# A graph network's first layer: its scatter-add goes to two tables in HBM in place of four

## What is computed

```
gate = sigmoid(edge_feature @ W_edge + b_edge)[:, 0]
xp = x @ W_node.T + b_node
row, col = src, dst
msg = gate[:, None] * xp[col]
summed = segment_sum(msg, row, num_segments=12500)
cnt = segment_sum(ones, row, num_segments=12500)
x = layernorm(x + summed / max(cnt, 1.0))
```

## Time and profile before

| | us |
|---|---|
| median of 3 runs | 13932.11 |
| lowest and highest | 13918.93 and 13973.37 |
| span of the profiled execution | 13968.9 |
| of it, first start of a scatter (L691) | 218.3 |
| last start of a scatter | 3319.1 |
| last of the three adds of the tables ends | 3364.5 |

### The profile page before, as it was taken

How to read it: one execution, slowest core, us unless ns; L and a number is a source line. 1 busy time by engine, 2 the same in 40 slices (tenths; PEclk the granted TensorE clock), 3 DMA queues, 4 the chain that set the end, 5 groups by cost and what they waited for, 6 DMA issues and landing times.

```text
span 13968.9 us, 160913 instructions
## 1 busy us (share of the span) xinstructions
PE 6562.6 (47%) x39606; PEld 5620.6 (40%) x39607; DVE 6528.4 (47%) x13212; ACT 1918.5 (14%) x3205; POOL 8846.4 (63%) x8158
## 2 busy tenths in 40 slices
PE   5777787784555555688600000085333333333333
PEld 5777777774555555677500000074111111111111
DVE  6444444444566666799700000198344345434335
ACT  0111111111222222566400000000000000000000
POOL 3888888884677777200177777500777774777774
PEclk7666666665777777899755555598555556555556
DMA  5333333332444444333222222232111111111111
GB/s 99 18 18 18 18 18 18 18 18 58 119 127 126 125 127 126 109 99 98 62 49 54 54 54 54 54 97 74 39 39 39 39 39 38 39 39 39 39 39 31
DMA packets 851731, 827.56 MB, mean 59 GB/s; under 512 B 630365, under 2 KB 636739, under 8 KB 849108
## 3 DMA queue, kind: packets, MB, share of 16 engines
q0 software_dynamic: 450064, 387.16, 18.7%
q1 hardware_dynamic: 398412, 436.75, 9.9%
q10 hardware_dynamic: 3218, 3.20, 0.1%
HBM read 571.36 MB, written 255.06 MB: 59 GB/s over the span
## 4 chain that ended last, share of the span: by engine, by line
POOL 51%; issue 22%; PE 10%; DMA 9%; DVE 5%; SPq 1%; DVEq 1%; POOLq 0%; ACT 0%; ACTq 0%
POOL tab L734 21%; POOL aux L708 10%; POOL lane_tab L691 9%; DMA lane_tab<-rows,idx 8%; POOL buf_b L708 6%; POOL acc_w L708 4%; PE ps L1122 3%; PE ps L1233 2%; PE ps L1169 1%; PE ps L1155 1%; DVE buf_b L1700 1%; SPq L558 1%; PE ps L1011 1%; POOL t_first_tab L719 1%; PE ps L1118 1%
## 5 line engine op out<-in xcount | busy, mean ns | idle before, releaser
L734 POOL DMA_INDIRECT tab<-gcn_tab,idx x3136 | 2984.5, 952 | 1780.3 <-issue 1777.6
L691 POOL DMA_INDIRECT lane_tab<-rows,idx x1664 | 2595.7, 1560 | 616.1 <-issue 614.6
L1134 PE MATMUL ps<-ident_b,zero_b 128*128 128x512 bf16 x1664 | 771.6, 618 | 2918.8 <-issue 1620.3
L1774 DVE TENSOR_REDUCE buf_d<-ps 128x512 f32<-128x1536 f32 x416 | 731.2, 1758 | 2301.0 <-PE ps L1138 2301.0
L708 POOL DMA_INDIRECT aux<-att_tab,idx x1568 | 1485.7, 948 | 477.8 <-issue 477.8
L1134 PEld LDWEIGHTS ps<-ident_b,zero_b 128*128 128x128 bf16 x1664 | 182.0, 128 | 3281.1 <-issue 1886.4
L708 POOL DMA_INDIRECT buf_b<-src_tab,idx x832 | 842.7, 1013 | 464.9 <-issue 253.4
L1036 PE MATMUL ps<-ident,srcg 128*128 128x128 f32 x3328 | 713.9, 401 | 663.4 <-DVE srcg L1398 663.3
L708 POOL DMA_INDIRECT acc_w<-src_tab,idx x832 | 815.4, 980 | 253.6 <-issue 248.1
L1036 PEld LDWEIGHTS ps<-ident,srcg 128*128 128x128 f32 x3328 | 661.0, 304 | 711.5 <-DVE srcg L1398 711.4
L1212 PE MATMUL ps<-ident,acc_w 128*128 128x128 f32 x13 | 3.0, 426 | 1953.9 <-ACT idx L831 1953.9
(11 more groups left out here) (307 smaller groups left out, 14192.6 us busy)
## 6 DMA issues: line engine op xcount, KB each, us to landing
y_stash<-buf_c SPq DMA_DIRECT2D x208, 512.0 KB
tab<-y_stash SPq DMA_DIRECT2D x208, 512.0 KB, 3.3
aux<-in_edge_attr_dram SPq DMA_DIRECT2D x1696, 32.0 KB
h_stash<-aux SPq DMA_DIRECT2D x196, 264.0 KB, 2.0
tab<-gcn_tab,idx POOLq DMA_INDIRECT x3136
buf_c<-h_stash SPq DMA_DIRECT2D x156, 264.0 KB, 2.7
lane_tab<-rows,idx POOLq DMA_INDIRECT x1664, 3.2
aux<-att_tab,idx POOLq DMA_INDIRECT x1568
```

The source lines that it names most:

```text
L691: pool.indirect_dma_start(lane_tab[k][:, :], bass.IndirectOffsetOnAxis(ap=idx[:, b, u:u + 1], axis=0), rows[:, b, u, 0:D1], None, compute_ ...
L734: pool.indirect_dma_start(g_rows[k][:, u, :], None, table[:, :], bass.IndirectOffsetOnAxis(ap=idx[:, k % RING, u:u + 1], axis=0)).then_inc ...
L1134: pe.matmul(ps[:, 4 * (q % 2) + c, :].rearrange("p (k f) -> p k f", f=P), zero_b[:, :], bc(ident_b[:, :].unsqueeze(1), [P, 4, P]), start=T ...
L1774: dve.tensor_reduce(g_sum[b], parts(4 * b), AX.X, ALU.add).then_inc(s.split_joined, 1)
```

## The change

LANES becomes 2. Two tables are kept, zeroed, filled and read back. Step u of a turn goes to table u % 2, so that each scatter waits for the landing of the last but one; the values waited for follow from LANES. `l0_landed` is raised at the turn's second wait in place of its fourth. Behind the stage two loads and one add remain of four loads and three adds; the semaphore `lane_again` and the use of `tab` for a third table go. Nothing else differs.

```diff
--- before.py
+++ after.py
@@ -39,7 +39,7 @@
 NOWHERE = 1 << 20
 TRASH = NP
 SROWS = NP + P
-LANES = 4
+LANES = 2
 RING = 4
 TURNS = S // G // RING
 TT = -(-T // (G * RING))
@@ -281,8 +281,6 @@
             "zeros_made",
             "lane_done0",
             "lane_done1",
-            "lane_done2",
-            "lane_done3",
             "l0_sources",
             "l0_source_rows",
             "l0_gated_hot",
@@ -298,9 +296,6 @@
             "lanes_done",
             "lane_in0",
             "lane_in1",
-            "lane_in2",
-            "lane_in3",
-            "lane_again",
 
             "l1_indices",
             "l1_rows_used",
@@ -402,7 +397,7 @@
             "result_stored",
         ]
         s = namedtuple("Semaphores", NAMES)(*[sem(n) for n in NAMES])
-        fill = [s.lane_done0, s.lane_done1, s.lane_done2, s.lane_done3]
+        fill = [s.lane_done0, s.lane_done1]
         y_in = [s.l1b_y_in0, s.l1b_y_in1, s.l1b_y_in2, s.l1b_y_in3]
         h_in = [s.l2b_h_in0, s.l2b_h_in1, s.l2b_h_in2, s.l2b_h_in3]
         e_in = [s.edges_in0, s.edges_in1, s.edges_in2, s.edges_in3]
@@ -414,7 +409,7 @@
             engine.wait_ge(rows_in[q], i * (G * 16) + (TURNS_BEFORE[stage] + 1) * (G * 16))
 
         h_stored = [s.h_stored0, s.h_stored1, s.h_stored2, s.h_stored3]
-        lane_in = [s.lane_in0, s.lane_in1, s.lane_in2, s.lane_in3]
+        lane_in = [s.lane_in0, s.lane_in1]
 
         def bc(ap, shape):
             return ap.to_broadcast(shape)
@@ -530,11 +525,8 @@
             def lane_rows(k):
                 return lane_tab[k][0:NP, :].rearrange("(p w) f -> p w f", p=P)
 
-            tab_l = tab_flat[:, 0:W * D1].rearrange("p (w f) -> p w f", f=D1)
-            for k, to in ((0, acc[:, :, :]), (1, aux[:, :, :]), (2, tab_l)):
+            for k, to in enumerate((acc[:, :, :], aux[:, :, :])):
                 sp.dma_start(to, lane_rows(k)).then_inc(lane_in[k], 16)
-            sp.wait_ge(s.lane_again, 1)
-            sp.dma_start(aux[:, :, :], lane_rows(3)).then_inc(lane_in[3], 16)
 
 
             def store_tab(table, n, base):
@@ -686,12 +678,12 @@
                     for u in range(G):
                         k = u % LANES
 
-                        pool.wait_ge(fill[k], i * 64 + (16 + 32 * b + 16 * (u // LANES)))
+                        pool.wait_ge(fill[k], i * (2 * G // LANES * 16) + (16 + G // LANES * 16 * b + 16 * (u // LANES)))
                         pool.sem_inc(s.l0_landed if u == LANES - 1 else s.passed, 1)
                         pool.indirect_dma_start(lane_tab[k][:, :], bass.IndirectOffsetOnAxis(ap=idx[:, b, u:u + 1], axis=0),
                                                 rows[:, b, u, 0:D1], None, compute_op=ALU.add).then_inc(fill[k], 16)
             for k in range(LANES):
-                pool.wait_ge(fill[k], 16 + 64 * ITER)
+                pool.wait_ge(fill[k], 16 + 2 * G // LANES * 16 * ITER)
             pool.sem_inc(s.lanes_done, 1)
 
             def gathers(table, to, idx_ready, free, turns=TURNS, stored=None):
@@ -1440,14 +1432,8 @@
                                           bc(col_b[:, start:end].unsqueeze(2), [P, end - start, D]), ALU.mult).then_inc(ready, 1)
 
 
-            tab_l = tab_flat[:, 0:W * D1].rearrange("p (w f) -> p w f", f=D1)
             dve.wait_ge(lane_in[0], 16)
             dve.wait_ge(lane_in[1], 16)
-            link(dve.tensor_tensor(acc[:, :, :], acc[:, :, :], aux[:, :, :], ALU.add))
-            dve.sem_inc(s.lane_again, 1)
-            dve.wait_ge(lane_in[2], 16)
-            link(dve.tensor_tensor(acc[:, :, :], acc[:, :, :], tab_l, ALU.add))
-            dve.wait_ge(lane_in[3], 16)
             link(dve.tensor_tensor(acc[:, :, :], acc[:, :, :], aux[:, :, :], ALU.add))
             sums_d = acc[:, :, 0:D]
             last_d = acc[:, :, D:D1].rearrange("p w a -> p (w a)")
```

## The result

| | before | after |
|---|---|---|
| median of 3 runs, us | 13932.11 | 14208.33 |
| lowest and highest | 13918.93 and 13973.37 | 14170.66 and 14214.58 |
| span of the profiled execution | 13968.9 | 14206.5 |

A forecast was written before the change was run, and what follows sets the result against it. The prediction took POOL's stream of scatters as the bound. Scatter waits +274 us, join -17.4 and zero fills 0 gave +257 us on 13,932.1, so 14,189 us, range 14,110 to 14,290.

The forecast's parts named there:

- The bound, and who follows it: Scatter stage: POOL's stream of scatters, 1.865 us a step, is the bound; ScalarE and TensorE only wait longer.
- The queue's cushion of two scatters: POOL's queue, four tables: two scatters stand decoded all the time, the wait met 4.19 us before the new start.
- The landing, 3.19 us: Scatter stage: a scatter lands 3.19 us after its instruction's start, also with two tables.
- The price, 0.83 us from wait to start: POOL's empty queue: 0.83 us from met wait to scatter start, ends 0.75 and 0.87; the term is +274 us.
- Stepping the two streams: Scatter stage, two tables: starts never closer than 1.845 us, so stepping gives 3,378 us in place of 3,361.
- The loop's end and the additions: POOL's queue: additions, branch and wait for copied rows fit in the sequencer's other 1.5 us, cost 0.
- The join, -17.4: Behind the scatter stage: one add at L1446 remains and ends at 3347.12 in place of 3364.51, -17.4 us.
- The zero fills: Kernel's beginning: two of four 3.2 MB fills go, none ends a wait on the path; 0, at most 0.5 us gain.
- Sum: Whole kernel: 274 - 17.4 = +257 us, a span of 14,226 and a median of 14,189 us, 1.8% slower.
- The idle time before the scatters: Sign in the changed kernel's scatter group: idle time up from 616 to about 890 us.
- Rival A: Scatter stage: sequencer's 0.53 us done before the wait is met, start at 3.51 us, kernel at 13,940; chance 0.08.
- Rival B: Idle POOL is slow: each scatter 0.17 us more, kernel at 14,347; chance 0.08, shared with other losses above 360 us.

The follow-up runs named there:

- e2: Three tables in place of the changed kernel's two, GpSimd loop written out, two adds in the join: 13,912.31 us median, ratio 0.9995.
- e5: The changed kernel with one table, a join of one load and no add: 17,468.05 us, a single run.
- e3: The changed kernel with two tables and the GpSimd loop written out in full: 14,170.31 us median, ratio 1.018.
- e4: Changed kernel, loop written out, wait held by the scatter itself; only each turn's second scatter keeps separate waits and a count: 13,966.75 us median, ratio 1.0033.
- e6: Changed kernel with one table, loop written out, wait held by the scatter, except each turn's first with a count: 16,767.57 us, a single run.
- e7: Changed kernel, loop written out, all landing waits held by scatters, ScalarE waiting for both tables itself, no POOL count: 13,945.89 us median, ratio 0.9992.
- e1: The kernel before with four tables, each scatter also waiting for the landing of the last but one: 14,202.32 us median, ratio 1.0203.

## Why the prediction was right, and where it was not

- **The bound, and who follows it**: right. POOL set the stage's end before and after, and the others' waits grew by what it lost.
- **The queue's cushion of two scatters**: right, and e2 shows it from the other side: a wait for the third before is still hidden.
- **The landing, 3.19 us, unchanged by two tables**: right; 3.2 in the middle in all nine traces, with one to four tables.
- **The price, 0.83 us from wait to start: mis-sized.** It is 0.74 (e5), just below the 0.75 that I kept as lower end, and nearer to the gathers of the earlier trace rows at 9742.97 (0.76) than to the first scatter. The 0.83 is what the stage's first scatter costs: the changed kernel's first one shows it again, a wait met at 219.02 and a start at 219.85, and in all nine traces it is 0.83 to 0.86. My step "I take 0.83, since it is the same instruction" was wrong; a stage's first scatter is a worse guide than a like instruction of which many have run before. It is not the first pass through the queue's code that costs: in e3 every scatter is an instruction of its own that runs once, and most start 0.74 us after their wait too. What it is, is open. By the stepping rule with the durations and landings of before, 0.74 gives 3,307 us and not 3,378, a loss of 203 and not 274.
- **Late starts: missing in the sum.** What made up for it is that the empty queue lays bare what the cushion had covered. In the changed kernel 14 scatters, each 112 after the last, start 2.11 us after their wait, and 26, mostly 59 apart, 1.48, where it is 0.74 otherwise. The row of 2029.92 above is such a one. There were 28 scatters of over 2.0 us in the engine, where 6 had been. The rule with after's own durations and landings gives 3,327, with these 40 late starts put in as well 3,362, and 3,363 was measured: 203 + 20 + 36 = 259. I had cost everything else in the queue at 0, on the ground that the sequencer has 1.5 us to spare; these are no part of what it does in the loop (e3), but they fall on it.
- **Stepping the two streams, "the streams can't drift freely"**: its form is borne out by that 3,362 against 3,363. Its worth of 17 us in the sum was measured by no run.
- **The loop's end and the additions, 0**: right (e3).
- **The join, -17.4**: -17.3. That aux may come sooner without the third load was a guess in the range; it doesn't (17.55 us against 17.36).
- **The zero fills, 0**: right to 2 us; the first scatter started no sooner.
- **Sum**: +257 forecast, +238 between the two profiled executions, +276 between the medians, which lie on different sides of the second layer's two lengths. That 14,189 is so near to 14,208 is partly luck: a price too high by 71 us, late starts and longer landings left out with 56, and a median before with the shorter second layer beside one after with the longer.
- **The idle time before the scatters, 616 to about 890 us**: 906.7, but this sign was read from a figure with 109.5 us of idle time before the first scatter in it, which grew to 138.0 with two zero fills gone. Between scatters it grew by 262 us, and I had +274.
- **Rival A** asked whether the 0.53 us of the sequencer can be done before the wait. In the changed kernel it is not, because the wait is its own instruction ahead of the scatter. e4, e6 and e7 show that it can be where the scatter holds the wait: 0.27 from landing to start, 3.46 for the pair, under 3.69, and the loss is gone. The rival's mechanism is real, but not in this program. The figure of the Trainium skill that I set beside it ("DMA: Bandwidth & Descriptors", section "Anatomy of one DMA — SWDGE (gpsimd) path": some 50 ns for the dispatch) fits neither form: 0.50 us of work before the wait, and 0.27 behind it. Nearer to what e4, e6 and e7 show is the Trainium skill's "Perfetto Trace Analysis", section "DMA Instruction — SWDGE (GPSIMD)": there an instruction is decoded first and waits for its semaphores afterwards, in a queue, while the sequencer is ready for the next. The traces agree with the order for a wait that the scatter holds. That the sequencer goes on meanwhile they don't bear out: in e6 the queue's next step behind a turn's last scatter waits for a copy that ended some 24 us earlier, and yet it stands 0.03 us behind the landing that this scatter waits for, in 205 of 207 turns.
- **Rival B**, a POOL that is slow when it was idle: fell. The scatters behind idle time take 1.54 us like the others.

What is open: what the late starts are, and why the first scatter takes 0.83 us from wait to start. The late starts recur after fixed numbers of scatters, with the loop or without it, and not after fixed times: with one table (e5), where a step takes twice as long, they stand 113 and 60 scatters apart, with four tables and the wait of two (e1) 110 and 57. That speaks for something that is used up by the DMAs issued and made new, but the count changes a little with the kernel, and nothing was tried to show it.

## What to carry to other kernels

Where waits are a queue's own instructions, count how many steps ahead they are met: as long as the engine has prepared work in its queue a wait is free (here when it was met 2.3 us before the start was due, with three tables). Met 0.48 us before, with two, it was too late, as 0.74 us go by from wait to start: each pair of scatters lost the difference, 0.26, and every rare delay that the work ahead had covered comes on top. A count put between a wait and a DMA keeps the DMA from being prepared during the wait; held by the DMA itself, the same wait was 0.27 us from landing to start. Take the price of a start from a place where many such instructions have already run, and not from a stage's first one.

## What was not expected of the hardware

- A scatter with nothing ahead of it starts 0.77 us after the landing it waits for when the wait is an instruction of its own, 0.27 us when it holds the wait (e5, e6).
- Starts come late by 1.4 us every 112 scatters and by 0.7 us about every 59 (2.11 and 1.48 us from wait to start for 0.74); those of 2.11 at the same places in the loop and in the written-out form.
- Scatters that add to two tables of 3.3 MB in turn land as soon as scatters at the same pace to four: 3.2 us in the middle (the changed kernel, e1). One table gave 3.2 as well, at half the pace (e5).
